# A two-layer decoder on one core: first transfers in order of use, and attention mixes of 18 columns

## The reference, cut to what matters

```python
x = ln(x + self_attention(x))          # 16 heads of 8, rotary, causal over 64 keys
x = ln(x + cross_attention(x, ctx))    # 16 heads, layer norm on each head's q and k
x = ln(x + fp4_ffn(x))                 # gate, up, down; weights and activations rounded to FP4
x = ln(x + linear_attention_block(x))  # convolutions, linear attention, a GELU MLP
x = ln(x + causal_cross_attention(ctx, x))
x = ln(x + experts(x))                 # 8 experts, the best two of each token
```

## Time and profile before

| | |
|---|---|
| median of three runs | 839.5 us (839.31 to 840.3) |
| the profiled execution | 838.08 us |
| its span, first to last instruction | 836.3 us |
| mean granted TensorE clock | 0.90 of full |
| read from and written to HBM | 8.17 MB, 1.05 MB |

### The profile page before, as it was taken

One profiled execution on the slowest core, in us unless ns is written; L12 is line 12 of the kernel. 1 busy time (PEld: TensorE's weight loads), 2 busy tenths in 40 slices (PEclk: granted clock), 3 DMA queues, 4 the chain that ended last, 5 costly groups with the idle time before them and its releaser, 6 DMA issues.

```text
span 836.3 us, 13289 instructions
## 1 busy us (share of the span) xinstructions
PE 654.9 (78%) x5081; PEld 434.0 (52%) x5081; DVE 562.1 (67%) x1492; ACT 335.1 (40%) x544; POOL 132.3 (16%) x248
## 2 busy tenths in 40 slices
PE   1798479675788796999958955877768979889995
PEld 0467347443454474566635743564435536646663
DVE  7486767899676765555548695778977657555555
ACT  0663445221755552422226533632238446332220
POOL 1302400202015111000023042021120340100002
PEclk9999779787899898999979996996779979999998
DMA  8000000000000000000000000000000000000000
GB/s 302 40 2 27 25 2 2 1 0 1 1 1 1 1 2 1 1 1 0 1 28 1 3 1 1 2 1 1 0 2 1 1 0 2 2 1 0 1 1 25
DMA packets 8867, 10.11 MB, mean 12 GB/s; under 512 B 1240, under 2 KB 7776, under 8 KB 8288
## 3 DMA queue, kind: packets, MB, share of 16 engines
q1 hardware_dynamic: 8800, 9.22, 3.3%
HBM read 8.17 MB, written 1.05 MB: 11 GB/s over the span
## 4 chain that ended last, share of the span: by engine, by line
PE 59%; DVE 24%; ACT 8%; issue 4%; POOL 3%; another core or an unknown queue 1%; DMA 1%; SPq 0%; POOLq 0%; DVEq 0%
PE ps L783 14%; PE ps L545 8%; PE ps L774 7%; PE ps L481 6%; PE ps L500 5%; PE ps L467 2%; POOL s_rs L1518 2%; ACT s_probs L902 2%; DVE s_r L1087 1%; DVE s_work L1063 1%; DVE s_work L1073 1%; DVE s_work L1076 1%; DVE s_x L1098 1%; PE ps L512 1%; PE ps L623 1%
## 5 line engine op out<-in xcount | busy, mean ns | idle before, releaser
L1515 POOL TENSOR_TENSOR s_rs<-s_mv,eps 128x1 f32<-128x1 f32 x96 | 18.9, 199 | 548.2 <-DVE s_mv L1093 368.7
L1014 ACT ACTIVATE s_k<-ps,eb 128x512 f32<-128x512 f32 x64 | 44.0, 687 | 132.9 <-PE ps L783 132.8
L1450 DVE SCALAR_TENSOR_TENSOR s_pT<-ps,eb,s_k 128x512 f32<-128x512 f32 x64 | 48.0, 749 | 57.0 <-ACT s_k L1014 53.7
L1117 DVE TENSOR_REDUCE s_row_max<-ps 128x16 f32<-128x1024 f32 x48 | 58.6, 1221 | 41.0 <-PE ps L500 41.0
L545 PE MATMUL ps<-s_v,s_pT 128*64 128x108 f32 x1536 | 82.0, 261 | 2.0 <-ACT s_headsT L893 1.7
L545 PEld LDWEIGHTS ps<-s_v,s_pT 128*64 128x64 f32 x1536 | 73.5, 138 | 11.0 <-issue 10.5
L882 ACT ACTIVATE s_pT<-ps 128x512 f32<-128x512 f32 x96 | 56.8, 594 | 47.2 <-PE ps L481 46.3
L481 PE MATMUL ps<-tabs,s_probs 128*128 128x128 f32 x384 | 63.7, 292 | 14.1 <-ACT s_probs L902 12.8
L774 PEld LDWEIGHTS ps<-wo,s_pT 128*128 128x128 f32 x512 | 61.7, 192 | 17.7 <-issue 12.4
L783 PE MATMUL ps<-s_xT,wg 128*128 128x512 f32 x128 | 69.3, 624 | 1.5 <-DVE s_pT L1450 1.1
L783 PE MATMUL ps<-s_xT,wu 128*128 128x512 f32 x128 | 67.4, 609 | 0.0
(11 more groups left out here) (221 smaller groups left out, 1125.4 us busy)
## 6 DMA issues: line engine op xcount, KB each, us to landing
mats<-in_mats SPq DMA_DIRECT2D x1, 1216.0 KB, 9.4
s_cin<-in_ctx SPq DMA_DIRECT2D x4, 256.0 KB, 4.4
s_xin<-in_x SPq DMA_DIRECT2D x4, 256.0 KB, 4.8
wg<-in_wg SPq DMA_DIRECT2D x1, 1024.0 KB
wu<-in_wu SPq DMA_DIRECT2D x1, 1024.0 KB
wo<-in_wo SPq DMA_DIRECT2D x1, 1024.0 KB
out_x<-s_x SPq DMA_DIRECT2D x4, 256.0 KB, 2.4
fc<-in_fc SPq DMA_DIRECT2D x2, 256.0 KB
```

The lines of the kernel that those rows point to most:

```text
L1014: act.activation(h.esg[:, n % 2, :], h.ps[:, 0, 0:TOK], ACT.Silu, bias=eb[:, 0, n:n + 1]).then_inc(h.e_silu, 1)
L1117: dve.tensor_reduce(h.row_max[:, t % 2, :], s3, AX, ALU.max).then_inc(h.max_here, 1)
L1450: dve.scalar_tensor_tensor(h.ehid[:, (n // 2) % 2, n % 2, :], h.ps[:, 1, 0:TOK], eb[:, 1, n:n + 1], h.esg[:, n % 2, :], ALU.add, ALU.mult) ...
```

## The change

Four things change.

1. **Transfers.** SP opens the first pass before it issues any transfer, then issues in the order FP4 gate/up, tables, tokens and context of stream 0, the first six square matrices, FP4 down, stream 1's tokens and context, identity, mask, constants, the other 13 matrices, biases, MLP weights, router and expert weights. Each group has a semaphore of its own, and each engine waits at the first use, inside the loop, in place of the one wait for everything.
2. **FP4 weights.** They have buffers of their own (before they were laid in the keys' buffer of stream 1). DVE still rounds them before the loop. PE's nine transposes and ACT's three copies move into the loop, ahead of the FFN of stream 0, and are done in both passes.
3. **Constants.** The setting of `v2` and `hq`, and the two small sums for `cw1`, move from DVE to POOL.
4. **The mix** takes 18 columns a pair in place of 108, and `v2` loses its padding.

```diff
@@ sync
-            sp.dma_start(tabs[:, :], tables_in).then_inc(tabs_here, 16)
-            sp.dma_start(cols[:, :], cols_in).then_inc(tabs_here, 16)
-            sp.dma_start(fp4_gu, fp4_gu_in).then_inc(fp4_here, 16)
...
-            for dst, src in late:
-                sp.dma_start(dst, src).then_inc(late_here, 16)
+            open_pass()
             for h in streams:
                 sp.sem_inc(h.stored, 16)
-            open_pass()
+            sp.dma_start(fp4_gu[:, :], fp4_gu_in.rearrange("p c n -> p (c n)")).then_inc(fp4_here, 16)
+            sp.dma_start(tabs[:, :], tables_in).then_inc(tabs_here, 16)
+            load(0, 0)
+            sp.dma_start(mats[:, 0:MATS_FIRST, :], mats_in[:, 0:MATS_FIRST, :]).then_inc(mats_here, 16)
+            sp.dma_start(fp4_d[:, :], fp4_d_in).then_inc(fp4_d_here, 16)
+            load(0, 1)
+            sp.dma_start(identb[:, :], identb_in).then_inc(mask_here, 16)
+            sp.dma_start(cmask[:, :], cmask_in).then_inc(mask_here, 16)
+            sp.dma_start(cols[:, :], cols_in).then_inc(cols_here, 16)
+            sp.dma_start(mats[:, MATS_FIRST:, :], mats_in[:, MATS_FIRST:, :]).then_inc(more_mats_here, 16)
...
@@ tensor, the mix
-                                v0 = (2 * t + b) * H + 2 * j
-                                ins = pe.matmul(h.ps[S * b:S * b + S, 3, 18 * j:18 * j + WINDOW * (DK + 1)],
+                                ins = pe.matmul(h.ps[S * b:S * b + S, 3, 18 * j:18 * j + 18],
                                                 h.pT[:, t % 2, j, S * b:S * b + S],
-                                                h.v2_all[:, v0:v0 + WINDOW, :].rearrange("p h e -> p (h e)"),
+                                                h.v2[:, 2 * t + b, 2 * j:2 * j + 2, :].rearrange("p h e -> p (h e)"),
@@ tensor
+            def turn_fp4_weights(h):
+                pe.wait_ge(fp4_w_ready, 1)
+                for c in range(2 * KC):
+                    pe.transpose(h.ps[:, c // 4, tile(c % 4)], fp4_gu[:, tile(c)], ident)
+                for c in range(KC):
+                    ins = pe.transpose(h.ps[:, 2, tile(c)], fp4_d[:, tile(c)], ident)
+                ins.then_inc(fp4_w_turned, 1)
+
             def ffn(h):
+                if h is streams[0]:
+                    turn_fp4_weights(h)
                 yield
@@ tensor, before the loop
-            pe.wait_ge(tabs_here, 48)
-            pe.wait_ge(fp4_w_ready, 1)
...
-            pe.wait_ge(late_here, 16 * LATE)
+            pe.wait_ge(tabs_here, 16)
@@ scalar
+            def take_fp4_weights(h):
+                act.wait_ge(fp4_w_turned, 1)
+                act.activation(gu_w[:, 0:4 * P], h.ps[:, 0, :], ACT.Copy)
+                act.activation(gu_w[:, 4 * P:6 * P], h.ps[:, 1, 0:2 * P], ACT.Copy)
+                act.activation(d_w[:, :, :], h.ps[:, 2, 0:KC * P].rearrange("p (c n) -> p c n", n=P),
+                               ACT.Copy).then_inc(fp4_w_here, 1)
+
             def ffn(h):
+                if h is streams[0]:
+                    take_fp4_weights(h)
                 yield from take_x(h, 3, 3)
...
-            act.wait_ge(late_here, 16 * LATE)
@@ vector, before the loop
-            for h in streams:
-                dve.memset(h.hq[:, :, :], 0.0)
-                dve.memset(h.v2_all[:, :, :], 0.0).then_inc(v_zeros_set, 1)
...
-            dve.wait_ge(fp4_here, 32)
+            dve.wait_ge(fp4_here, 16)
             at_once(ffn_weights(streams[0]))
-            dve.wait_ge(late_here, 16 * LATE)
+            dve.wait_ge(tabs_here, 16)
@@ gpsimd, before the loop
             for h in streams:
+                pool.memset(h.v2[:, :, :, :], 0.0).then_inc(v_zeros_set, 1)
+            pool.wait_ge(v_zeros_set, 2)
+            for k, h in enumerate(streams):
+                pool.memset(h.v2[0:S, :, 0::2, DK:DK + 1], 1.0).then_inc(v_ones_set, 1)
+                pool.wait_ge(v_ones_set, 2 * k + 1)
+                pool.memset(h.v2[S:P, :, 1::2, DK:DK + 1], 1.0).then_inc(v_ones_set, 1)
+                pool.wait_ge(v_ones_set, 2 * k + 2)
+            for h in streams:
+                pool.memset(h.hq[:, :, :], 0.0)
                 pool.memset(h.vz[:, :, :, :], 0.0).then_inc(zeros_set, 1)
+            pool.wait_ge(cols_here, 16)
+            pool.tensor_scalar(cw1[:, 0:1], col("cpe1_w1"), 1.0, None, ALU.add)
+            pool.tensor_scalar(cw1[:, 1:2], col("cpe2_w1"), 1.0, None, ALU.add).then_inc(conv_mids_set, 1)
             pool.wait_ge(consts_set, 2)
-            pool.wait_ge(late_here, 16 * LATE)
```

More of the change, by code:

```diff
@@ L341, in decoder @@
         streams = [stream(k) for k in range(STREAMS)]
-        fp4_gu = placed(streams[1].k4, 0, 2 * KC, P)
-        fp4_d = placed(streams[1].k4, 2 * KC * P, FFN_PAD)
+        fp4_gu = sb("fp4_gu", [P, 2 * KC * P])
+        fp4_d = sb("fp4_d", [P, FFN_PAD])
         def col(name):
@@ L367, in decoder @@
         tabs_here = sem("tabs_here")
+        cols_here = sem("cols_here")
+        more_mats_here = sem("more_mats_here")
         mask_here = sem("mask_here")
         fp4_here = sem("fp4_here")
-        late_here = sem("late_here")
+        fp4_d_here = sem("fp4_d_here")
+        biases_here = sem("biases_here")
+        fc_here = sem("fc_here")
+        experts_here = sem("experts_here")
         last_stored = sem("last_stored")
@@ L439, in _ @@
+            for dst, src in ((fc1[:, :], fc1_in), (fc1b[:, :], fc1b_in), (fc2[:, :, :], fc2_in)):
+                sp.dma_start(dst, src).then_inc(fc_here, 16)
+            for dst, src in ((router[:, :], router_in), (eb[:, :, :], eb_in), (wg[:, :, :], wg_in), (wu[:, :, :], wu_in),
+                             (wo[:, :, :], wo_in), (bout[:, :], bout_in)):
+                sp.dma_start(dst, src).then_inc(experts_here, 16)
             with sp.Fori(0, PASSES - 1) as c:
@@ L725, in fc1_part @@
                     yield
+                    if m == 0:
+                        pe.wait_ge(fc_here, 48)
                     if m >= 2:
@@ L993, in linear_block @@
                     yield
+                    if m == 0:
+                        act.wait_ge(fc_here, 48)
                     act.wait_ge(h.block_pe, BLOCK_PE[f"fc1_done {m + 1}"])
@@ L1026, in network @@
                 yield from experts(h)
[L1028 to L1033, removed]
-            act.wait_ge(late_here, 16 * LATE)
+            act.wait_ge(tabs_here, 16)
             with act.Fori(0, PASSES):
@@ L1484, in network @@
                 yield from experts(h)
-            for h in streams:
-                dve.memset(h.hq[:, :, :], 0.0)
-                dve.memset(h.v2_all[:, :, :], 0.0).then_inc(v_zeros_set, 1)
-            dve.wait_ge(v_zeros_set, 2)
-            for h in streams:
-                dve.memset(h.v2[0:S, :, 0::2, DK:DK + 1], 1.0)
-                ins = dve.memset(h.v2[S:P, :, 1::2, DK:DK + 1], 1.0)
-            ins.then_inc(v_ones_set, 1)
-            dve.wait_ge(tabs_here, 48)
-            dve.tensor_scalar(cw1[:, 0:1], col("cpe1_w1"), 1.0, None, ALU.add)
-            dve.tensor_scalar(cw1[:, 1:2], col("cpe2_w1"), 1.0, None, ALU.add).then_inc(conv_mids_set, 1)
-            dve.wait_ge(fp4_here, 32)
+            dve.wait_ge(fp4_here, 16)
             at_once(ffn_weights(streams[0]))
-            dve.wait_ge(late_here, 16 * LATE)
+            dve.wait_ge(tabs_here, 16)
             with dve.Fori(0, PASSES):
```

41 lines of the change are left out of this document (18 added, 23 removed).

## The result

The kernel after takes 826.06 us (median of four runs, 825.0 to 828.05) against 839.73 of the kernel before (four runs): a ratio of 0.984, 95% interval 0.981 to 0.987. It is faster by 13.7 us, where 29 were forecast: the time lies in the range of 800 to 828, but at its upper end. Two executions of the kernel before in a later round, at 1602 and 3377 us, lay far off all others and are in no ratio or median here.

A forecast was written before the change was run, and what follows sets the result against it. PE was taken to bound the attention stretches, with DVE next, and the loop's start to wait for the last of 8 MB; start -15, turned weights +2 and mix -16 sum to -29, giving 810.5 us, 8 in 10 within 800 to 828.

The forecast's parts named there:

- The mix: Attention stretches: 18 columns save 26 us of PE, 60% of it on the path, -16 us, bounds 0 and -24.
- the Trainium skill's rule on LDWEIGHTS: Rival in the mix: 32 weight loads one after the other keep it as long as today; 826.5 us, chance 0.02.
- DVE takes over: Rival in the attention stretches: DVE or the fixed order takes over, the mix saves nothing; 826.5 us, chance 0.15.
- PE without a gap in the chain: Attention stretches: PE goes from scores to probabilities to mix with no gap, the argument against DVE taking over.
- The clock falls: Rival in the attention stretches: granted clock falls, kernel ends slower; 870 us at a half share, chance 0.08.
- The start: Before the loop: DVE's first loop instruction moves from 30.34 to 15.4 us; -15 us taken, bounds -12 and -17.
- DVE sets the start: Start: DVE's rounding, ending at 15.2 us, and not PE's query projection, decides when DVE enters the loop.
- queries are there before 15: Start: PE's query projection, 5.1 us for both streams, is done before 15 us, ahead of DVE.
- The turned weights: Loop, end of cross attention: nine transposes and three copies cost +1 us a pass, +2; bounds 0 and +6.8.
- The constants on POOL: Start: POOL's memsets take about 7 us, over by 8, before anything needs them, and cost nothing.
- The waits at first use: Inside the loop: some ten waits per pass, already satisfied, cost below 1 us together.
- Slower or faster: Whole kernel: faster 0.90, slower 0.08, a difference under 0.2% (1.7 us) 0.02.

The follow-up runs named there:

- e9: The kernel before, with DVE's maximum of the scores taken over the first 32 of 64 keys: 840.3 us, ratio 0.999.
- e10: The kernel after, with DVE's maximum of the scores taken over the first 32 of 64 keys: 813.3 us, ratio 0.968 to the kernel before.
- e2: The kernel after with the old 108-column mix and padded buffer put back, so the start alone: 832.5 us, ratio 0.989 to the kernel before.
- e11: The kernel before with a mix of 36 columns and nothing else: 834.5 us, ratio 0.993.
- e12: The kernel after with a 36-column mix and a useless 384-column matmul in the FP4 block: 820.0 us, ratio 0.975 to the kernel before.
- e3: The kernel after with a mix of 54 columns: 817.2 us, ratio 0.970 to the kernel before.
- e5: The kernel after with a mix of 36 columns: 816.5 us, ratio 0.975 to the kernel before.
- e14: The kernel after with the 108-column mix and no FP4 turning in the loop, those weights a constant: 828.5 us, ratio 0.987 to the kernel before.
- e1: The kernel before with the 18-column mix and nothing else: 840.2 us, ratio 0.9985.
- e7: The kernel after with a useless 256-column matmul ahead of each 18-column mix: 834.5 us, ratio 0.995 to the kernel before.

## Why the prediction was wrong, point by point

**The mix, the step that failed.** The sum took 60% of 26 us. Its first half held: L691's 29 ns carried over, a mix went from 1.63 to 1.04 us where about 1.1 was forecast, and PE's busy time of it fell by 27.0. The rival that the prediction took from the Trainium skill's rule on LDWEIGHTS, a mix that stays at 1.6 us, did not come true: the trace shows 1.04. What failed is "I take 60% of 26, -16": alone, the mix is worth 1.3 us (0 within its interval), and on top of the new start 4 to 6. In the profiled execution the six attentions became 6.8 us shorter, and the rest of the kernel 8.6 us longer. The bound below, 0, was right, and the value inside was too bold for two reasons.

- *DVE takes over*, a rival with 0.15, in its mechanism. DVE at 72% of the attention stretches looked like room for 23 us, and it was not. e9 and e10 show it: less of DVE's work is worth nothing before and 12.7 us after, 7.7 of them in the attentions. "PE without a gap in the chain", the argument against, was read from 50 to 60 us; from 40.6 to 48.6 the chain was on DVE twice. That the rival's time, 826.5, is also the measured one is in part luck: it has 13 us for start and turning, where e2 gives 7 to 9, and nothing for the mix, which gives 4 to 6 on top.
- *The clock falls*, a rival with 0.08, placed in the middle of the attention stretches and priced as a loss of 43 us if it came. It came mostly outside them or at their ends, as after 132 us, with 55 us more at half clock, and it does not make the kernel slower than before; it takes back what the mix gave. 36 columns at the same price give 9.5 us back, none of them in the attentions. In the sum itself the clock stood at nothing outside the attentions. Within most kernels too the executions with the higher clock are the faster ones: in e11 829.97 us at a mean of 0.884 and 840.58 at 0.872, in e12 814.38 at 0.905 and 823.25 at 0.883. The prediction had each rival alone; both came, in part.

**The start.** The transfers did what was forecast, and the term was a little large: -13.5 for -14.9. "DVE sets the start" and "queries are there before 15" did not hold. DVE's rounding took 12.1 us for 11.1, nearly all of the difference in one operation of 1.13 us (it took 0.19 before), but PE's query projection ended 0.5 us later still. PE's part, taken as 5.1 us, was 8.2, from 8.57 to 16.80, with the wait for stream 1's tokens and the slow projections in it. The windows show a granted clock of 1.00 there, so why these projections took nearly twice their time is open. In e3 and e5 the rounding ended last instead, so the two are close. Behind that the whole start is worth 7 to 9 alone. What it loses lies, by e2's trace, mostly in stretches of lower clock and not in the turning.

**The turned weights** were +2 with a bound of 6.8; e2 and e14 give between 0 and 4, which agrees but is not sharp. Their place was seen, not that PE might be at half clock there: the nine took 1.92 us, from 137.11 to 139.03, where 1.1 to 1.3 were forecast.

**The constants on POOL** were done at 7.20 us, as forecast (before 8). They probably did cost DVE its one long operation, see the last section. **The waits at first use** cost nothing that shows: no transfer stands among the long waits of the loop after stream 1's inputs.

**Slower or faster.** Faster, with 0.90, was right, and the range of 800 to 828 held the time. The gain was 13.7 us for 29. By e2, start and turning gave 4 to 6 us less than forecast, and the mix 10 to 12 less.

## What to carry to other kernels

Before paying for fewer columns, ask what the columns cost: here 36 and 54 cost TensorE no more than 18, and where its granted clock hangs on its work they are worth something. Before forecasting a share of a saved engine's time, take work from the next engine instead and see what that is worth; where it is worth nothing now and much after, the next engine has become the limit. Look at where in the kernel the gain falls before giving all of it to that engine. And read the whole chain of a stretch, not ten microseconds of it. Neither a higher mean clock nor a lower busy time is the goal by itself: each counts only where TensorE is what the chain goes through.

## What the runs showed of the hardware

- The same 32-instruction mix costs the same busy time with 18, 36 and 54 float32 columns (55.0, 53.6, 54.5 us in 1536 instructions), 59.3 with 72 and 82.0 with 108. TensorE's next instruction starts about every 29 ns with 64-column weights in alternate halves.
- In a stretch with a granted clock of 0.54, the 18-column mix took 1.90 us, and at 1.00 it takes 1.11 in the same view (1.04 in the chain).
- The first projections of the kernel after took 1.91 and 1.54 us for two instructions of 512 columns until 16.6 us, and 1.02 from then on, with a granted clock of 1.00 in the windows of both.
- A DVE operation of 48 elements took 1.13 us beside POOL's memsets, from 5.17 to 6.30, where it took 0.19 before; POOL's `hq` memset ended at 6.26. The neighbours in time went at their usual pace, so this reads as one stall, not a slow stretch. All twelve kernels with the new start show it, with 1.13 to 2.18 us; the four with the old start (before, e1, e9, e11) show 0.19. In each of the twelve the operation ends 0.04 or 0.05 us behind the end of a POOL memset, the second of `hq` or, in e3, e7 and e12, the next one of `vz`. No run took the memsets away by themselves. The Trainium skill ("SBUF — State Buffer", section "SBUF: two separate sides") says that a DVE operation in a two-port mode and a GpSimd one share a port pair as an exclusive lock, and that the later one waits in full. These ends agree with it, but that only this one operation was held, while memsets ran from 3.96 to 7.20, no run here explains.
- The executions of one kernel spread by up to 1%: 837.0 to 845.3 for the kernel before over all rounds, 812.7 to 820.6 for e3. The small differences here (36 against 54 columns, the fillers) stay inside it.
